# Integers turned as 16-bit halves, a router in four matmuls, and a reordered head of attention

## The reference

```python
x = x + smooth_quant_expert(layernorm(x), gu, ctx)     # int8 rounding of both operands, silu, twice
x = x + bitlinear_ffn(layernorm(x), w1, w2, w3)        # weights rounded to -1, 0, 1
x = x + cross_attention(layernorm(x), ctx, mask, Wq, Wk, Wv, Wo)   # 16 heads, 8 key/value heads
logits = layernorm(x) @ router.T                       # 8 experts, all held here
topk_w = softmax(top_k(logits, 2))                     # two weights that sum to 1
x = x + shared_mlp(y) + routed_mlp(y) * sum(topk_w * (topk_idx < 8))
```

## Time and profile before

| what | value |
|---|---|
| median of 3 runs | 402.36 us (402.32 to 403.2) |
| the profiled execution | 402.94 us |
| its span | 401.2 us |
| granted TensorE clock, mean | 0.998 |
| instructions | 8419 |
| TensorE matmul busy | 388.4 us, 97% |
| VectorE busy | 299.9 us, 75% |
| ScalarE busy | 232.5 us, 58% |
| GpSimd busy | 165.6 us, 41% |

### The profile page before, as it was taken

The page is one execution under the profiler, slowest core; times in us unless marked ns, Lnnn a source line. Parts: engine busy times, 40 slices in busy tenths (PEclk is TensorE's granted clock), DMA queues, the critical chain, the costliest instruction groups (busy, mean ns, idle before and its releaser), DMA issues.

```text
span 401.2 us, 8419 instructions
## 1 busy us (share of the span) xinstructions
PE 388.4 (97%) x2986; PEld 363.8 (91%) x2986; DVE 299.9 (75%) x973; ACT 232.5 (58%) x616; POOL 165.6 (41%) x263
## 2 busy tenths in 40 slices
PE   8898999999999999999999999999999999999996
PEld 7788898998899989999999989998999889999896
DVE  4787979789867889777766989787767776665634
ACT  1897777775643566666553566766444666664342
POOL 2114666774633345235353435235443323242331
PEclk9999999999999999999999999999999999999999
DMA  7999100000000200000000100000000000000000
GB/s 236 327 347 395 56 31 2 2 2 0 3 2 0 83 0 2 2 1 2 2 26 2 57 1 2 0 2 2 1 28 2 0 2 0 2 2 0 29 2 26
DMA packets 15113, 16.86 MB, mean 42 GB/s; under 512 B 1568, under 2 KB 14048, under 8 KB 15072
## 3 DMA queue, kind: packets, MB, share of 16 engines
q1 hardware_dynamic: 15072, 16.33, 12.6%
HBM read 15.28 MB, written 1.05 MB: 41 GB/s over the span
## 4 chain that ended last, share of the span: by engine, by line
PE 77%; DVE 10%; ACT 5%; DMA 3%; issue 2%; POOL 1%; SPq 1%; DVEq 0%; POOLq 0%
PE bank_qa L388 10%; PE bank_o L632 7%; PE bank_u L615 7%; PE bank_pt L599 7%; PE bank_s L579 6%; PE bank_s L388 5%; PE bank_o L636 3%; PE bank_u L619 3%; PE bank_s L587 3%; PE bank_pt L388 3%; PE bank_s L503 3%; DMA wq_raw<-in_wqT 3%; PE bank_u L712 2%; ACT prob L967 2%; PE bank_pt L503 2%
## 5 line engine op out<-in xcount | busy, mean ns | idle before, releaser
L1263 POOL TENSOR_SCALAR prob<-prob,row_inv,valid_b 128x256 f32<-128x256 f32 x128 | 71.1, 565 | 93.8 <-DVE row_inv L1627 93.7
L967 ACT ACTIVATE prob<-prob,row_min 128x256 f32<-128x256 f32 x128 | 64.1, 502 | 55.1 <-DVE row_min L1619 55.1
L1632 DVE TENSOR_TENSOR pt_lo<-bank_pt,pt_hi 128x512 fp32r<-128x512 f32 x64 | 43.6, 682 | 14.6 <-ACT pt_hi L920 14.6
L1619 DVE CUSTOM_DVE_ANT_0 prob<-bank_s,masked 128x256 f32<-128x256 f32 x128 | 48.7, 419 | 1.8 <-PE bank_s L587 0.8
L1274 POOL TENSOR_TENSOR act_lo<-act_raw,act_hi 128x256 fp32r<-128x256 f32 x32 | 24.3, 758 | 46.1 <-ACT act_hi L1032 46.1
L599 PE MATMUL bank_pt<-ident,prob 128*128 128x128 f32 x256 | 42.1, 277 | 1.0 <-POOL prob L1263 0.7
L1638 DVE TENSOR_TENSOR ut_lo<-bank_u,ut_hi 128x512 fp32r<-128x512 f32 (+1 forms) x36 | 22.7, 631 | 24.2 <-ACT ut_hi L920 23.8
L920 ACT ACTIVATE pt_hi<-bank_pt 128x512 fp32r<-128x512 f32 x64 | 37.5, 586 | 5.1 <-PE bank_pt L599 4.6
L388 PE MATMUL bank_qa<-xt_hi,a_hi 128*128 128x256 f32 x126 | 39.5, 313 | 0.4 <-DVE qa_lo L1600 0.4
L599 PEld LDWEIGHTS bank_pt<-ident,prob 128*128 128x128 f32 x256 | 29.6, 141 | 8.6 <-POOL prob L1263 4.1
L388 PE MATMUL bank_qa<-xt_lo,a_hi 128*128 128x256 f32 x126 | 35.2, 279 | 0.0
(11 more groups left out here) (327 smaller groups left out, 1206.4 us busy)
## 6 DMA issues: line engine op xcount, KB each, us to landing
wq_raw<-in_wqT SPq DMA_DIRECT2D x4, 512.0 KB, 7.7
wo_raw<-in_wo SPq DMA_DIRECT2D x4, 512.0 KB, 8.2
w_raw<-in_w12T SPq DMA_DIRECT2D x2, 704.0 KB, 7.8
gate_raw<-in_gateT SPq DMA_DIRECT2D x2, 576.0 KB, 7.6
up_raw<-in_upT SPq DMA_DIRECT2D x2, 576.0 KB, 10.1
down_raw<-in_downT SPq DMA_DIRECT2D x2, 576.0 KB, 12.6
x<-in_x SPq DMA_DIRECT2D x4, 256.0 KB, 6.3
guT<-in_guT SPq DMA_DIRECT2D x4, 256.0 KB, 3.7
```

The costliest lines, as they stand in the source:

```text
L967: act.activation(row, row, ACT.Exp, scale=-1.0, bias=row_min[:, h % 2, t:t + 1], accum_out=row_sum[:, h % 2, t:t + 1]).then_inc(S["s_exp"], 1)
L1263: pool.tensor_scalar(row, row, row_inv[:, h % 2, t:t + 1], valid_b[:, 0:1], ALU.mult, ALU.mult).then_inc(S["s_norm"], 1)
L1619: dve.tensor_tensor_reduce(out=prob[:, h % 2, t, :], in0=src[:, t * T:(t + 1) * T], in1=masked[:, :], scale=1.0, scalar=3.0e38, op0=ALU.ad ...
L1632: dve.tensor_tensor(pt_lo[:, :, cols], bank["pt"][:, :].rearrange("p (s t) -> p s t", s=2), f32(pt_hi[:, :, cols]), ALU.subtract).then_inc ...
```

## The change

Four things are changed. The turns of rounded values read the low 16 bits of each fp32 value as bf16 (the identity by its high halves) and write 16-bit values, which are then converted from int16; MAGIC is no longer subtracted. The router's hi and lo weights lie side by side as 16 columns: four matmuls instead of six give hi x hi and lo x hi in separate rows, and VectorE adds the halves after the turn. The order at the head of attention is changed: at every head row_inverses stand ahead of mix_lo and row_minima ahead of routed_residual; and where n is 7 (batches 0 and 1) the queries of heads 2 and 3 stand ahead of the scores of head 1, and the split of these queries ahead of the last chunk's act_hi and act_lo. Last, route_top, its tanh and route_sum come one, one and two chunks later. Batch 2 has only five chunks at once, so its call of route_sum at chunk 5 doesn't take place, and comb keeps batch 1's value.

```diff
-        router_hi = sb("router_hi", [P, ND, NR], F32R)
-        router_lo = sb("router_lo", [P, ND, NR], F32R)
+        router = sb("router", [P, ND, 2 * NR], F32R)
+        router_hi, router_lo = router[:, :, 0:NR], router[:, :, NR:2 * NR]
+        scores8 = sb("scores8", [P, NT, NR])
...
+        def low_half(ap):
+            return ap.bitcast(BF16)[:, 0::2]
+
+        def high_half(ap):
+            return ap.bitcast(BF16)[:, 1::2]
...
-                        dst = bank["x0"] if j < 2 else bank["x1"]
+                        dst = bank["x0" if j < 2 else "x1"][:, 0:D].bitcast(BF16)
                         for k in range(ND):
                             last = pe.transpose(dst[:, k * 256 + (j % 2) * P:k * 256 + (j % 2 + 1) * P],
-                                                qw[:, j, k * P:(k + 1) * P], ident[:, :])
+                                                low_half(qw[:, j, k * P:(k + 1) * P]), high_half(ident[:, :]))
...
-                for k in range(ND):
-                    last = split_mm(bank["x1"][0:NR, 0:T], router_hi[:, k, :], router_lo[:, k, :],
-                                    yt_hi[:, k, :], yt_lo[:, k, :], k == 0, k == ND - 1)
+                for n, (cols, y) in enumerate(((2 * NR, yt_hi), (NR, yt_lo))):
+                    for k in range(ND):
+                        last = pe.matmul(bank["x1"][0:cols, 0:T], router[:, k, 0:cols], y[:, k, :],
+                                         start=(n == 0 and k == 0), stop=(n == 1 and k == ND - 1),
+                                         skip_group_check=True)
...
                     if not last and c == ATT_SCORES[b] + 1:
                         pe.wait_ge(S["ffn_prod"], FFN_CHUNKS * b + n - 1)
+                        if n > 6:
+                            queries(b + 1, 2)
+                            queries(b + 1, 3)
                         scores(b + 1, 1)
-                        queries(b + 1, 2)
-                        queries(b + 1, 3)
+                        if n <= 6:
+                            queries(b + 1, 2)
+                            queries(b + 1, 3)
...
-                act.activation(qT[:, 0:2, :].rearrange("p a n -> p (a n)"), bank["x0"][:, :], ACT.Copy,
-                               bias=-MAGIC).then_inc(S["q_bf"], 1)
+                act.copy(qT[:, 0:2, :].rearrange("p a n -> p (a n)"), bank["x0"][:, 0:D].bitcast(I16)
+                         ).then_inc(S["q_bf"], 1)
...
+                    if not last and p == n - 1 and n > 6:
+                        queries_hi(b + 1, 1)
                     ffn_high(b, p)
-                    if p == (ROUTE_LATE + 2 if last else 2):
+                    if p == (ROUTE_LATE + 2 if last else 3):
...
                     before(h)
+                    if 1 <= h < H - 1:
+                        row_inverses(b, h + 1)
                     if h >= 1 and h - 1 == mix_heads(mix_unit(h - 1))[-1]:
                         mix_lo(b, mix_unit(h - 1))
-                    if 1 <= h < H - 1:
-                        row_inverses(b, h + 1)
                     probs_lo(b, h)
+                    if h + 2 < H:
+                        row_minima(b, h + 2)
                     if h == 0 and b > 0:
                         routed_residual(b - 1)
-                    if h + 2 < H:
-                        row_minima(b, h + 2)
...
-                hold()
-                for t in range(NT):
-                    last = dve.max(top8[:, t, :], bank["x1"][:, t * NR:(t + 1) * NR])
+                halves = bank["x1"][:, 0:2 * NT * NR].rearrange("p (t w n) -> p t n w", t=NT, w=2)
+                link(dve.tensor_reduce(scores8[:, :, :], halves, AX.X, ALU.add))
+                for t in range(NT):
+                    last = dve.max(top8[:, t, :], scores8[:, t, :])
...
-                    if p == (ROUTE_LATE + 1 if last else 1):
+                    if p == (ROUTE_LATE + 1 if last else 2):
                         route_top(b)
-                    if p == (ROUTE_LATE + 3 if last else 3):
+                    if p == (ROUTE_LATE + 3 if last else 5):
                         route_sum(b)
...
+                if not last and n > 6:
+                    queries_lo(nxt, 1)
                 dve.wait_ge(S["ffn_hi"], FFN_CHUNKS * b + n)
                 r = (n - 1) % 3
                 dve.tensor_tensor(act_lo[:, r, :], act_raw[:, r, :], f32(act_hi[:, r, :]), ALU.subtract
                                   ).then_inc(S["ffn_lo_last"], 1)
-                if not last:
-                    row_minima(nxt, 1)
-                    queries_lo(nxt, 1)
...
+                    row_minima(nxt, 1)
+                    if n <= 6:
+                        queries_lo(nxt, 1)
```

More of the change, by code:

```diff
@@ L31 @@
 BF16 = mybir.dt.bfloat16
+I16 = mybir.dt.int16
 U8 = mybir.dt.uint8
@@ L226, in build @@
         guT = sb("guT", [P, ND, 2 * I])
-        logits = qw[0:NR, 0, :]
+        logits = qw[0:2 * NR, 0, :]
         top8 = sb("top8", [P, NT, NR])
@@ L673, in route_turn @@
                 for t in range(NT):
-                    last = pe.transpose(bank["x1"][:, t * NR:(t + 1) * NR], logits[0:NR, t * P:(t + 1) * P],
-                                        ident[0:NR, 0:NR])
+                    last = pe.transpose(bank["x1"][:, t * 2 * NR:(t + 1) * 2 * NR], logits[:, t * P:(t + 1) * P],
+                                        ident[0:2 * NR, 0:2 * NR])
                 last.then_inc(S["route_t"], 1)
@@ L1081, in batch @@
                         exps(b + 1, 0)
-                    queries_hi(b + 1, 1)
+                    if n <= 6:
+                        queries_hi(b + 1, 1)
                     exps(b + 1, 1)
```

10 lines of the change are left out of this document (6 added, 4 removed).

## The result

The changed kernel takes 396.11 us (median of 4 runs, 395.64 to 397.99), the kernel before in the same set 402.78 us (4 runs). The profiled execution took 396.23 us with a span of 394.5 us, against 402.94 and 401.2: 6.7 us too.

What follows compares the result with a forecast made beforehand. TensorE was taken to set the pace except in VectorE-bound stretches at the head of attention. Router 0.9, turns 1.5, heads 0.1 + 0.8, reciprocals 0.7 sum to 4.0 us: 402.36 to 398.4 us, own range 397.7 to 399.1.

Steps and rivals of the forecast that it cites:

- I took two readings: Starting step: count TensorE instructions that go away, and find where TensorE stands still because VectorE, ScalarE or GpSimd is late.
- Rival 2: VectorE's stretches are softer than read and early reciprocals give TensorE its 1.6 us: 396.8 us; chance 0.14.
- turns: 16-bit turns cost 0.055 us for 0.109: 0.43 us in each of batches 1 to 3, 0.2 in the prologue; 1.5 us.
- batch 3's head: Head of attention, batch 3: route_sum gone, cxT_lo clear of GpSimd, residual behind the minima; 0.8 us, ends 0.5 and 1.2.
- the heads of batches 1 and 2: Head of attention: rearranged order and residual behind the minima net 0.06 us a batch beyond the router's gain, 0.1 in all.
- the reciprocals: Row reciprocals ahead of mix_lo: 0.6 us at heads 3 to 11 of batch 3, 0.13 in batch 0; sum 0.7 us.
- Router: Six matmuls become four, 0.23 us per batch on the chain, reduction costed at nothing: 0.9 us.
- "gone" and "0.8": Sign in batch 0: TensorE's wait at head 3 gone and head 5's grown to 0.8 us.
- rival 4: Slower: a weight load picking every second half-word of qw could be slow; at 0.4 us a turn 404.0 us; chance 0.05.
- rival 1: 16-bit turns are no faster: 1.5 us back, 399.9 us; the router's turns cited for it; chance 0.15.
- The first sign: Mix(0) to mix(0) shrinks by 0.7 us from batch 1 to 2; much other than that makes the forecast wrong.
- the second: Mix(0) to mix(0) shrinks by 1.5 us from batch 2 to 3; much other than that makes the forecast wrong.

Runs made afterwards that it cites:

- experiment 1: Kernel before with an unused tensor of 64 bytes per partition where the change puts scores8, no instruction changed: 401.56 us, ratio 0.9966.
- experiment 2: Changed kernel with scores8 allocated behind all other tensors, so that all lie where they lay before the change: 399.02 us, ratio 0.9899.
- experiment 8: Kernel before with row_inverses ahead of mix_lo alone: 401.7 us, ratio 0.997.
- experiment 14: Kernel before with the router's pick later alone (route_top behind chunk 2, tanh at chunk 3, route_sum behind chunk 5): 402.56 us, ratio 0.9986.
- experiment 10: Changed kernel with the router's pick (route_top, tanh, route_sum) back in the chunk blocks where it stood: 397.97 us, ratio 0.988.
- experiment 9: Kernel before with the routed residual behind the row minima of head 2 alone: 401.68 us, ratio 0.9983.
- experiment 7: Changed kernel with scores of head 1 again ahead of the queries of heads 2 and 3, and their split moved back, in batches 1 and 2: 396.62 us.
- experiment 6: Changed kernel with scores8 moved from ahead of w12 to behind comb, putting scores and queries at 64 bytes too: 396.76 us, ratio 0.9846.
- experiment 12: Changed kernel without the swap at the head, laid out so that w12 and w3, too, lie 64 bytes off their operands: 395.84 us, ratio 0.9823.
- experiment 11: Kernel before with 32 unused bytes per partition where the change puts scores8: 402.41 us, ratio 1.0.
- experiment 13: Kernel before with 96 unused bytes per partition where the change puts scores8: 402.77 us, ratio 0.9984.

## Why the prediction was wrong

**The step that failed** is the first one: "I took two readings: how many TensorE instructions go away, and where TensorE stands still". A third was needed: how fast the instructions that stay follow each other. The part on the router costs its matmuls, its copy and its reduction, but not that its new buffer scores8, 64 bytes per partition, is allocated behind a, c, gate, up and down and ahead of w12, xt, yt, act and ut, and so moves one operand of most products against the other. That moved the feed-forward from 119.6 to 116.5 ns a matmul and the queries from 116.5 to 118.6. It is worth 1.20 us in the kernel before (experiment 1) and 1.73 in the changed one (experiment 2). Without it, the stretch gains 4.33 us; my terms for it sum to 3.86, and the kernel of experiment 2, 399.02 us, lies in the range. The rows were there to read: the chain of the kernel before has 1.36 us for twelve query matmuls and 1.44 us for twelve feed-forward ones (116.5 and 119.6 ns from start to start). I took 0.113 us from the first and didn't ask why two kinds of the same matmul differ.

Rival 2, which ended nearest to the time, is wrong as a mechanism: in batches 1 and 2 the early reciprocals gave nothing (experiment 8). And that my terms come so near to 4.33 is in part luck: turns and batch 3's head were too high by 0.3 and 0.1 us, the heads of batches 1 and 2 too low by 0.5 together, the reciprocals too low by 0.4.

**The terms.** The edits alone sum to 1.01 + 0.68 + 1.13 + 1.11 + 0.43 = 4.36 us for 4.33 together. They don't simply add all the same: the swap is not in the sum, and the pick is worth 0.43 us alone and 1.26 undone from the changed kernel.

Router: right at its place, 0.23 us four times. 0.2 of the 0.9 is lost ahead of mix(0) when nothing else changes (0.04, 0.03 and 0.13 us, where I had 0.2 a batch for a reduction without cover; it takes 0.18 us, the mean of four in the changed kernel). That it is at nothing with the pick moved fits the sum of experiment 14, which leaves 0.03 us, but no run shows it by itself.

Turns: the size was off, 0.35 us for eight instead of 0.43, for a spacing of 0.058 instead of 0.055 us and for seven steps instead of eight. The changed kernel's trace has 55 to 61 ns from turn to turn, 70 once a row, and eight in 0.45 us to the next operation. For the prologue, from the landing of wq_raw to mix(0), the gain is about 0.2, as forecast: 43.5 to 43.8 us in the profiles with old turns and without a clock fall, 43.3 to 43.4 with new ones. The remaining 0.5 us by which the changed kernel's profile is ahead there is the transfer, which ended at 17.30 instead of 17.79, within what it scatters.

Head of batches 1 and 2: off by 0.25 a batch (0.31 measured in experiment 2 for 0.06). That exps(1) comes 0.7 us later was wrong: on a common clock, shifted by the 1.26 us by which the changed kernel was ahead before the router, exps(1) starts at 142.91 for 142.57 before, 0.34 later. Two inputs failed. I costed queries_lo and act_lo at 0.60 each, but act_lo frees VectorE after 0.34 (140.85 to 141.19). In the kernel before it took 0.66 us, from 141.53, with GpSimd normalising beside it from 141.37; in the changed one it takes 0.42 and starts as GpSimd's pair (139.77, 1.09 us) ends. I took the duration from a row in which it was being disturbed. And I had the lead of the moved pick nowhere but in batch 3, while it is what takes most of the swap's cost away (experiments 10 and 14). Experiments 9 and 7 give the parts: 0.47 from the residual, minus 0.07 from the swap with the pick moved. I had set both at 0.5. The waits that were to come in place of mix(0)'s are small: 0.11 us between the last two matmuls of bank_o, 0.03 ahead of head 1's turns.

Head of batch 3: 0.67 for 0.8. cxT_lo fell to 0.42 us as forecast (304.75 in the changed kernel, GpSimd from 305.01), but queries(4) kept its wait (0.50 for 0.52) and mix(0) 0.30 of its 0.49. Experiment 10 against the changed kernel shows what the pair costs: cxT_lo takes 0.96 us where GpSimd's act_lo had started first and 0.42 where cxT_lo had. What I got wrong is that this happened in one place; it happened in three.

Reciprocals: the place was right, the size not: 1.13 us for 0.7. In batch 3 each of heads 5, 7, 9 and 11 had a second, smaller wait behind the one that I read, 0.17 to 0.19 for 0.10 to 0.12, and head 3 0.29 for 0.20. That VectorE-bound stretches give nothing held in batches 1 and 2. In batch 0 of the changed kernel head 3's wait halved (0.51 to 0.25) and head 5's grew from 0.17 to 0.34 with 0.20 between the turns behind it: given back, though less on both sides than "gone" and "0.8".

**Sums and readings.** Two things in the prediction are wrong without moving its forecast. The breakeven of rival 4 is 4.0/28 = 0.14 us a turn more than forecast (0.2 us a turn is the whole cost, not the excess), 0.3% slower comes at 0.19 more, and at 0.4 us a turn the time would be 398.4 + 28 x 0.345 = 408.1, not 404.0. And the 0.22 us of the router's two turns holds their latency: their starts lie 0.08 us apart, so they said less for rival 1 than I gave them.

**The signs.** Mix(0) to mix(0) shrank by 1.23 us from batch 1 to 2 and by 1.53 from 2 to 3, where 0.7 and 1.5 were forecast; with the tensors as before 0.80 and 1.24. The first sign thus failed in the changed kernel by just the pace of the matmuls. That the second came out, 1.53 for 1.5, is luck: without the pace it is 1.24.

**Open:** why distances of 0 and 96 bytes slow a matmul and 32 and 64 don't, and whether it is the matmul's own weights or those loaded for the next one that count. Inside a group they lie at the same distance. At two seams they don't: the last query matmul ahead of scores and the last one of the projection ahead of mix have their own weights at 64 and the next ones at 0 (modulo 128) in experiments 6 and 12, and the next start follows after 118.6 and 119.3 ns in the sixth, 116.0 and 114.9 in the twelfth (means of 47 and 32). Neither rule fits both. Nor why scores differ by 1.4 ns between two layouts with the same distance (experiments 6 and 12). Of the clock fall in the prologue I know what it costs, not what decides which run has it: the trace's record of the granted clock starts, at 1.00, at 4.3 to 5.3 us in six of the seven profiles with it, at 6.8 in the seventh and at 5.5 to 7.4 in the others. TensorE stood idle once between 14.8 and 16.9 us in all sixteen, for 1.0 to 1.6 us in those with the fall and 0.4 to 1.5 in the others, and nothing of this was varied.

## What to carry to other kernels

Read the spacing of like instructions from the chain before and after, group by group, even where no edit touches them; and when a change adds a buffer, see what it pushes along. Put a pad in the old kernel, or the new buffer at the end, before crediting the edit. When a median scatters, look where in the trace the scatter arises and measure past it: here a stretch that repeats to some hundredths of a microsecond resolved edits of 0.4 and 0.7 us which medians of 12 runs could not. An edit that is worth nothing alone can be worth something beside another: undo it in the changed kernel as well as make it in the old one. A wait that is "0.10" in one row may have a second part one row on; count from the same instruction to the same instruction of the next round.

## What the runs showed of the hardware

A 256-column fp32 matmul with a fresh 128x128 weight load followed the one before in 116.5 to 119.9 ns, by the byte distance between the moving operand and its weights in SBUF, counted modulo 128 and tried in steps of 32: with gate and up 119.6 ns at 0, 117.2 at 32, 116.5 at 64 and 119.9 at 96, with a 118.6, 117.0, 116.5 and 118.8. By the addresses of experiments 11 and 13, the fast 64 is 64 modulo 256 for yt and 192 for xt, the slow 96 is 96 and 224; 128 modulo 256 doesn't occur in these two groups. Others lie between, and up to 1.4 ns is left unexplained. Moving all tensors together by 64 bytes changed nothing (335.82 for 335.79 us over the stretch). Over this kernel that is 1.2 to 1.7 us, and 1.4 more for laying out the rest.

A transposing matmul on every second 16-bit half of fp32 data followed the one before in 0.055 to 0.061 us for 128 columns, about half of fp32's 0.109. No run has the same turns without the stride, so what the stride costs is not shown.

A VectorE subtraction of two 128x256 SBUF tensors took 0.96 us when a GpSimd subtraction had started 0.13 us before it (experiment 10), and 0.42 when it started 0.27 us ahead of GpSimd's (changed kernel).

The granted clock of TensorE fell once in the prologue, from 1.00 to 0.50 for 3.4 us (experiment 2: means of 0.65 over 18 to 21 us, 0.78 over 21 to 24), which costs 1.0 to 1.7 us of 400, in seven of sixteen profiles, over instructions that most of these kernels have in common.
